# A decoder of scan, depooling and experts: VectorE's side work cut into links and moved ahead of each slot's product

## The reference, cut to what matters

```python
# 1: a selective scan (width 1024, 16 states), per batch
xz = einsum(norm_w * x / rms(x), in_proj_w); xi, z = split(xz)
xc = silu(causal_conv(xi, 4 taps) + conv_b)
dt, Bm, Cm = split(einsum(xc, x_proj_w))
delta = softplus(dt @ dt_proj_w + dt_proj_b)
h_t = exp(delta_t * A) * h_(t-1) + delta_t * Bm_t * xc_t
y = (einsum(h, Cm) + xc * Dp) * silu(z)
x = layernorm(2 * x + y @ out_proj_w)
# 2: depooling of the context (16 x 750 x 1024, its first 512 columns)
x = layernorm(x + rmsnorm(x) @ W_in + b_in + scan over patches of rmsnorm(ctx), at each token's patch)
# 3: a mixture of 8 experts (512 to 2048 to 512), best expert per token, 448 rows each
x = layernorm(x + p * relu(x @ W1) @ W2), rows over the capacity without an expert
```

## Time and profile before

| | |
|---|---|
| median of 3 runs | 2866.54 us (2864.99 to 2867.36) |
| the profiled execution, its own time | 2864.87 us |
| its span, first to last instruction | 2863.1 us |
| VectorE busy (DVE) | 2266.5 us, 79% |
| TensorE busy (PE) | 2575.8 us, 90% |
| ScalarE busy (ACT) | 1704.4 us, 60% |
| GpSimd busy (POOL) | 1426.4 us, 50% |
| mean granted TensorE clock | 0.966 |

### The profile page before, as it was taken

The page is one execution under the profiler, slowest core; times in us unless marked ns, Lnnn a source line. Parts: engine busy times, 40 slices in busy tenths (PEclk is TensorE's granted clock), DMA queues, the critical chain, the costliest instruction groups (busy, mean ns, idle before and its releaser), DMA issues.

```text
span 2863.1 us, 36967 instructions
## 1 busy us (share of the span) xinstructions
PE 2575.8 (90%) x11808; PEld 2143.3 (75%) x11808; DVE 2266.5 (79%) x2456; ACT 1704.4 (60%) x3875; POOL 1426.4 (50%) x868
## 2 busy tenths in 40 slices
PE   4689998989899898989989899998769999999997
PEld 4577877778787776878778787877537888888886
DVE  4899999999999999999999999999933444434442
ACT  2576776867777786767678776767643333233331
POOL 0577667667667766766776766677710100000110
PEclk8799999999999999999999999999978999999999
DMA  7114202022020202212020211202033333343320
GB/s 211 58 39 150 75 17 75 22 74 72 26 82 18 75 17 79 61 38 82 18 74 18 78 52 46 75 17 68 16 124 114 114 117 121 108 139 115 114 101 13
DMA packets 90903, 208.35 MB, mean 73 GB/s; under 512 B 7742, under 2 KB 16574, under 8 KB 90498
## 3 DMA queue, kind: packets, MB, share of 16 engines
q1 hardware_dynamic: 81506, 184.61, 20.7%
q0 software_dynamic: 5120, 14.21, 1.6%
q10 hardware_dynamic: 4096, 7.34, 0.8%
HBM read 176.69 MB, written 29.98 MB: 72 GB/s over the span
## 4 chain that ended last, share of the span: by engine, by line
PE 46%; DVE 25%; issue 15%; POOL 7%; ACT 5%; DMA 1%; SPq 1%; DVEq 0%; POOLq 0%; ACTq 0%
DVE ring L1143 15%; PE ring L1444 12%; PE work L1444 11%; PE work L1277 8%; PE y L1430 7%; POOL arena L884 6%; DVE arena L984 2%; PE work L1256 2%; PE work L1293 2%; DVE arena L1145 2%; ACT ring L748 2%; PE work L1340 1%; DVE arena L944 1%; ACT arena L561 1%; DVE arena L992 1%
## 5 line engine op out<-in xcount | busy, mean ns | idle before, releaser
L884 POOL TENSOR_TENSOR arena<-arena 128x896 f32<-128x896 f32 x512 | 1058.9, 2088 | 581.9 <-PE y L1430 532.3
L1143 DVE TENSOR_TENSOR_SCAN ring<-ring,arena 128x896 f32<-128x896 f32 x512 | 1036.2, 2024 | 27.3 <-ACT ring L748 16.5
L748 ACT ACTIVATE ring<-arena,small 128x224 f32<-128x224 f32 x2048 | 794.5, 436 | 298.1 <-DVE arena L1145 297.6
L1430 PE MATMUL y<-arena,cst_sb 128*128 128x224 f32 x4096 | 868.9, 362 | 105.7 <-DVE arena L1145 105.7
L1430 PEld LDWEIGHTS y<-arena,cst_sb 128*128 128x128 f32 x4096 | 780.1, 194 | 166.2 <-DVE arena L1145 128.7
L1145 DVE TENSOR_TENSOR arena<-ring,arena 128x896 f32<-128x896 f32 x512 | 558.8, 1091 | 17.6
L1256 PE MATMUL work<-arena 128*128 128x224 f32 x1984 | 400.3, 358 | 52.9 <-DVE arena L984 47.1
L1256 PEld LDWEIGHTS work<-arena 128*128 128x128 f32 x1984 | 380.6, 193 | 61.0 <-DVE arena L984 52.6
L1200 DVE SCALAR_TENSOR_TENSOR hidden_lo<-work,hidden_hi 128x448 fp32r<-128x448 f32 x128 | 80.0, 625 | 387.9 <-ACT hidden_hi L788 387.9
L897 POOL DMA_INDIRECT out<-res,ids x32 | 42.7, 1333 | 670.1 <-DVE mst L1185 645.2
L788 ACT ACTIVATE hidden_hi<-work 128x448 fp32r<-128x448 f32 x128 | 69.7, 544 | 422.0 <-PE work L1444 422.0
(11 more groups left out here) (151 smaller groups left out, 2936.3 us busy)
## 6 DMA issues: line engine op xcount, KB each, us to landing
weights<-in_w SPq DMA_DIRECT2D x64, 1024.0 KB, 7.1
arena<-bc_rows SPq DMA_DIRECT2D x128, 448.0 KB, 4.5
arena<-in_ctx SPq DMA_DIRECT2D x16, 896.0 KB, 9.2
expert_rows<-x2e SPq DMA_DIRECT2D x1, 7224.0 KB, 31.9
xrow<-expert_rows SPq DMA_DIRECT2D x8, 903.0 KB, 11.1
arena<-in_xT SPq DMA_DIRECT2D x16, 448.0 KB, 9.5
arena<-in_x SPq DMA_DIRECT2D x16, 448.0 KB, 3.6
out<-arena ACTq DMA_DIRECT2D x32, 224.0 KB, 2.4
```

The source lines that it names most:

```text
L748: last = nc.scalar.activation(decays[s % 2][:, i * L:(i + 1) * L], delta[:, k, :], ACT.Exp, scale=a_neg[:, n:n + 1])
L884: nc.gpsimd.tensor_tensor(u[:, s % 4], dx[:, k:k + 1, :].to_broadcast([P, QN, L]), bc[:, 0, q * QN:(q + 1) * QN, :], ALU.mult).then_inc(u_ ...
L1143: nc.vector.tensor_tensor_scan(h, h, u_flat[:, s % 4, :], 0.0, ALU.mult, ALU.add).then_inc(scan_done, 1)
L1430: last = nc.tensor.matmul(o, ident, u[:, s % 4, i, :], start=False, stop=(q == Q - 1 and i == QN - 1))
```

## The change

1. `woven` gets a third part. On VectorE, `main(s)` is now only the scan; the side work of the slot follows; the product comes last, as `after(s)`.
2. VectorE's side work is cut at more places. Where a piece was a whole chain (`conv0`, `res0`, `norm2.1`, `best`, ...), each link with its wait is now a piece of its own (`conv0.1` to `.3`, `res0.0` to `.2`, `norm21.0` to `.2`, `best.0` to `.4`, ...).
3. All four tables are new, and the banks of `rank`, `dt0`, `t1`, `xatt0`, `xatt1` with them. A full step has VectorE's links in slots 0 to 7, 10 to 19, 21, 25, 26 and 30. ScalarE: the routed rows (`norm2.0`, `norm2.1`) from slots 0 and 3 to 4, silu from 12 to 11, the logarithms from 28 to 30. TensorE: `out0` from slots 7 to 9 to slot 6 whole, `out1` stays at 9. GpSimd: `delta1` and `delta2` to slot 7, `delta3` from 13 to 18, `scatter` from 21 to 24, `ctx` from 15 to 29, `delta0` from 30 to 32.
4. The scaling of the context weights goes from step -1 to slot 3 of step 0. In step -1 ScalarE's `skip` comes before the taps, the first z copies before silu and the squares behind it.
5. Steps 16 and 17 have tables of their own (`PE_DRAIN`, ...), and their jobs are dealt over four banks.

```diff
-        DVE_AT = {"norm2.1": 1, "conv0": 2, "conv1": 3, "conv2": 3.01, "gate3": 3.02, "best": 6, "mask": 6.01, "conv3": 10,
...
+        DVE_AT = {"norm21.0": 0, "norm21.1": 1, "norm21.2": 2, "w_xa": 3, "conv0.1": 3.01, "conv0.2": 3.02, "conv0.3": 3.03,
...
+        PE_DRAIN = in_order("""out0.0 out0.1 tx0 plug out0.2 out0.3 out1.0 out1.1 out1.2 out1.3 tx1 rt t0 rank t1 xatt0.0 xatt0.1
...
+        for s in (NB, NB + 1):
+            last_jobs = sorted(sum(jobs_of[s], []), key=lambda j: FIRST_PART(PE_DRAIN, j))
+            jobs_of[s] = [last_jobs[k::4] for k in range(4)]
...
-        def woven(side, main, scan):
+        def woven(side, main, scan, after=None):
...
                 while due < s + 1:
                     due = next(side, NEVER)
+                if scan and after:
+                    after(s)
...
-            def moments(e, k, h, step_of, name):
-
+            def moments(e, k, h, step_of, name, piece):
+
+                n = e * 8 + 2 * k
+                yield f"{piece}.1"
                 job_copied(dve, step_of, name)
-                n = e * 8 + 2 * k
                 nc.vector.bn_stats(st[:], r[0:H, h]).then_inc(mv_step, 1)
+                yield f"{piece}.2"
                 dve.wait_ge(mv_step, n + 1)
                 apart(dve)
                 nc.vector.bn_aggr(ln[:, k, 0:2], st[:]).then_inc(mv_step, 1)
...
-                dve.wait_ge(tap_ready, nxt * 4 + (j + 1))
-                bank, free = job_full(dve, b, f"xi{j}")
                 n = nxt * 16 + 4 * j
                 for tap in range(1, 4):
+                    yield f"conv{j}.{tap}"
+                    if tap == 1:
+                        dve.wait_ge(tap_ready, nxt * 4 + (j + 1))
+                        bank, free = job_full(dve, b, f"xi{j}")
...
-                    (corrections, pro), (patched, epi), (all_masks, first), (context_weights, first)) if there))
+                    (corrections, pro), (patched, epi), (all_masks, first), (context_weights, isinstance(b, int) and b == 0)) if there))
...
                     nc.vector.tensor_tensor_scan(h, h, u_flat[:, s % 4, :], 0.0, ALU.mult, ALU.add).then_inc(scan_done, 1)
+
+                def product(s):
+                    q = s % Q
+                    g = b * SLOTS + (s + 1)
+                    h = decays[s % 2]
                     dve.wait_ge(scan_done, g)
...
-                woven(side(b, par), main, stages(b)[2])
+                woven(side(b, par), main, stages(b)[2], product)
...
+                if isinstance(step, int) and step == NB and k >= 2 and name == jobs_of[NB][k][0]:
+                    pe.wait_ge(y_done, NB * PAIRS)
```

More of the change, by code:

```diff
@@ L273, in build_decoder @@
                                dt2 dt3 ssq""")
-        ACT_FIRST = in_order("""w_z tap0 tap1 tap2 tap3 square silu z0 z1 z2 z3 xp sp0 sp1 sp2 sp3 logs skip""")
-        DVE_FIRST = in_order("""conv0 w_xa conv1 conv2 conv3 masks0 masks1 masks2 masks3 masks4 masks5 masks6 masks7 corr0 corr1
-                                corr2 corr3""")
+        ACT_FIRST = in_order("""w_z skip tap0 tap1 tap2 tap3 z0 z1 z2 silu square xp z3 sp0 sp1 sp2 sp3 logs""")
+        DVE_FIRST = in_order("""conv0.1 conv0.2 conv0.3 conv1.1 masks0 masks1 conv1.2 conv1.3 conv2.1 conv2.2 conv2.3 conv3.1
+                                conv3.2 conv3.3 masks2 masks3 masks4 masks5 masks6 masks7 corr0 corr1 corr2 corr3""")
+        PE_DRAIN = in_order("""out0.0 out0.1 tx0 plug out0.2 out0.3 out1.0 out1.1 out1.2 out1.3 tx1 rt t0 rank t1 xatt0.0 xatt0.1
+                               xatt0.2 xatt1.0 xatt1.1 xatt1.2""")
+        ACT_DRAIN = in_order("""norm2.0 drop0 tx0 norm2.1 drop1 sq0 sq1 depool tx1 hx0 t0 hx1 t1 exp""")
+        DVE_DRAIN = in_order("""norm21.0 mask gate3 norm21.1 norm21.2 res0.0 patches res0.1 res0.2 res1.0 res1.1 res1.2 best.0
+                                best.1 best.2 best.3 best.4 chance.0 chance.1 slots.0 slots.1 slots.2 slots.3 norm20.0 norm20.1
+                                norm20.2""")
+        POOL_DRAIN = in_order("""ctx scatter""")
         FIRST_PART = lambda at, job: at[job if job in at else job + ".0"]
@@ L732, in logarithms @@
                     logs(b)
-                return together(ACT_AT if not first else ACT_FIRST, *(part() for part, there in (
+                return together(ACT_FIRST if first else ACT_DRAIN if not scan and not pre else ACT_AT, *(part() for part, there in (
                     (rows, tail), (routing, tail), (dropped, tail), (taps, pro), (silus, pro or scan), (channels, pro), (steps, pro),
@@ L870, in next_rows @@
                     nc.gpsimd.tensor_tensor(xn, xT, rinv[:, 1:2, :].to_broadcast([P, DC, L]), ALU.mult).then_inc(xn_ready, 1)
-                return together(POOL_AT, *(part() for part, there in (
+                return together(POOL_DRAIN if not scan and not pre else POOL_AT, *(part() for part, there in (
                     (late_steps, scan), (first_steps, pro), (scatter, tail), (context, epi), (next_rows, pre)) if there))
@@ L1008, in best_expert @@
                 nc.vector.tensor_reduce(rt[:, 0, :], logits, AX, ALU.max).then_inc(rt_step, 1)
+                yield "best.1"
                 dve.wait_ge(rt_step, n + 1)
@@ L1029, in slots_of @@
             def slots_of(b, n):
+                yield "slots.0"
                 bank, free = job_full(dve, b, "rank")
@@ L1127, in patched @@
                     patches(b, e)
-                return together(DVE_AT if not first else DVE_FIRST, *(part() for part, there in (
+                return together(DVE_FIRST if first else DVE_DRAIN if not scan and not pre else DVE_AT, *(part() for part, there in (
                     (masks, epi), (last_gate, epi), (gates, scan), (rows, tail), (convolutions, pro), (routing, tail), (residuals, epi),
-                    (corrections, pro), (patched, epi), (all_masks, first), (context_weights, first)) if there))
+                    (corrections, pro), (patched, epi), (all_masks, first), (context_weights, isinstance(b, int) and b == 0)) if there))
             def body(b, par):
@@ L1407, in next_rows @@
                     squares(b)
-                return together(PE_AT if not (isinstance(b, int) and b == -1) else PE_FIRST, *(part() for part, there in (
+                return together(PE_FIRST if pro and not scan else PE_DRAIN if not scan and not pre else PE_AT, *(part() for part, there in (
                     (inputs, pro), (gate_inputs, pro), (steps, pro), (routing, tail), (outputs, epi), (patches, epi),
```

50 lines of the change are left out of this document (26 added, 24 removed), and 23 rows, old and new, of tables (ACT_AT, DVE_AT, PE_AT).

## The result

The changed kernel takes 2760.13 us (median of 4 runs, 2759.17 to 2767.90) against 2866.51 for the kernel before in the same runs: a ratio of 0.9635, 95% interval 0.9617 to 0.9654. The forecast was 2771 us, range 2750 to 2812. The execution that was profiled is the longest of the four, 2767.90 us with a span of 2766.1. Compared with the one before (2863.1), the 97.0 us that went divide up so: first scan 13.6 earlier; steps 2 to 14 shorter by 71.7; steps 0, 1 and 15 by 1.3; from the end of the last product to the end of the span 10.3 (781.6 to 771.3).

A forecast was written before the change was run, and what follows sets the result against it. VectorE was taken as the bound, TensorE close behind. Thirteen full steps -63, steps 0, 1 and 15 -8, start -13.5, drain -10: 2864.9 - 94.5 = 2770.4, forecast 2771 us; own range 2755 to 2790, 2750 to 2812 with one rival.

The forecast's parts named there:

- Part 1: VectorE in full steps: links between scan and product, and cut chains, save 3.4 us a step, 122.8 to 119.4.
- The place: Links put between scan and product in 22 of 32 slots: 0.11 us each, 2.4 us a full step saved.
- Part 2: VectorE's waits in a full step, for ScalarE, TensorE and GpSimd: reordering cuts them from 3.0 to 1.4 us.
- the routed rows leave slot 0, where the 2.08 us wait is: Slot 0 of a full step: moving ScalarE's routed rows away leaves about 0.3 us of the wait for decays.
- Steps 0, 1 and 15: The three steps with fewer links: -1.5, -2 and -4.5 us, together -8, with the context scaling counted in step 0.
- Start and drain: Before the first scan, 13.5 us earlier (at 88); after the last sums, 10 us earlier, range 6 to 12.
- less 1 where TensorE no longer starts cold: Start, chain from TensorE's second z job to the last softplus: 1 us shorter, ending at 77.6 in place of 78.6.
- The other chain: Start: eight masks, two links, TensorE's second z job, then up to the last softplus; ends at 77.6, the masks' at 77.0.
- The gap can be hidden: Denies a rival: followers start 2.05 us after a scan regardless and cuts save nothing; 2817 us, chance 0.10.
- TensorE didn't take over: Denies a rival: TensorE's idle times of 2.25 and 3.78 us stay, a step can't go below 123.1; 2800 us, chance 0.17.
- it idles there as it does now: Full step: TensorE asks for conv0's bank before conv0 is through and still idles 2.25 us.
- the product is starved: Rival: links ahead of the product, worst at slot 3, delay TensorE, GpSimd and ScalarE; 2908 us, chance 0.04.

The follow-up runs named there:

- e2_product_first: Changed kernel with the product right behind its scan again and the links, still cut and on the new tables, behind the product: 2807.77 us, ratio 0.9791.
- e5_unrolled: Changed kernel with all steps written out, no loop over steps 2 to 11: 2761.59 us, ratio 0.9613.
- e3_weights_in_start: Changed kernel with the scaling of the context weights put back into step -1, behind conv0: 2778.06 us, ratio 0.9686.
- e4_old_drain: Changed kernel with steps 16 and 17 ordered by the common tables and dealt over two banks, as before: 2771.75 us, ratio 0.9666.
- e10_short_links: Kernel before, old tables, side work ahead of the product except in six slots with long pieces (2, 3, 10, 12, 26, 30): 2811.19 us, ratio 0.9806.
- e6_mask_reduce: Kernel before with the copy of a batch's two mask columns exchanged for a reduction over one element: 2841.19 us, ratio 0.9906.

## Why the prediction was right, and where not

The forecast missed the median by 11 us and the profiled execution, against which its sum was made, by 2.5 (2770.4 and 2767.9). Inside that sum some terms are right and others cancel: in steps 2 to 14 VectorE's own work fell by 2.4 us a step more than said, and its waits, which were to fall by 1.6, rose by 0.3. That the total came so near is in part luck.

**Part 1, right in kind, too small.** "Links 1.94 after scan": 1.93. The place gave 2.7 us a step where 2.4 stood. The cuts gave about 1.6 where 1.0 stood. VectorE alone went from 122.8 to 117.0 us (120.33 less 3.35 of waits over 0.2 us), not to 119.4. Of the 2.4 between, 0.3 are the place and 0.6 the cuts, and 1.4 are the mask copy, which I never looked at: its group is small, and its wait is in its duration, not in brackets. The rule of the Trainium skill (VectorE: DVE Perf Modes, The DRAIN you can't avoid) that the semaphore costs nothing doesn't carry over to this pair: it is 2.06 us from a scan to its waiting product and 1.93 to a free link, and over all slots this makes some 40 of the 45 us of `e2_product_first`.

**Part 2, the total near, two of its steps wrong.** Residual 1 waits no more, ScalarE is at most 0.6 late at slot 12 (0.7 said), and the fourth `u` fits. But the waits left are 3.35 us a step and not 1.4. The step "the routed rows leave slot 0, where the 2.08 us wait is" failed: that wait stands at steps 4, 6, 8 and 10 only, the turns of the loop, in both kernels, and it goes with the loop (`e5_unrolled`). I had read it in step 6 alone and put it down to the routed rows, so I took it as all but gone; it grew to 3.0 to 3.4. In the same four steps of this profile the additions at slot 4 wait 1.3 to 1.6 us for ScalarE, which is gone without the loop too. And the 0.4 for `u` "around slot 14" was 0.6 at slot 0, 1.4 to 1.6 at slot 11 and 0.2 at slot 14 in nine steps of thirteen. So the 5.5 us that a step lost are 5.8 less of VectorE's own and 0.3 more of waits, where 3.4 and 1.6 less stood.

**Steps 0, 1 and 15.** -8 said, -1.3 measured: +0.9, -1.9 and -0.3. Step 15 has 3.8 us of waits (for `u`, the decays and the logits) that I left out. Step 0 got 1.2 us from links between scan and product, but paid 1.6 for the scaling and 0.6 for a new wait for `u` at its end.

**Start and drain.** -13.5 said and 13.6 measured, the first scan at 87.7 for 88, by the chain of masks that was laid out; `e3_weights_in_start` gives it back. Only the term "less 1 where TensorE no longer starts cold" was wrong: its second z job took 5.29 us, at a granted clock of 0.60, where before it took 4.84. The other chain was done 1.4 us before 77.6 all the same, and the masks decided. -10 said for the drain: 9.9 at the last addition, 10.3 to the end; `e4_old_drain` gives 9 back.

```profile
51.09 5.29 PE L1290 MATMUL work<-arena 128*128 128x224 f32 x16 [16.28 <-DVE arena L1006]
```

**The rivals.** The gap can be hidden. TensorE didn't take over, though what is left is partly its doing. Both of the idle times on which that rival rested went, and so did the prediction's own "it idles there as it does now": over steps 2 to 14 TensorE waited for products and for the convolutions, as the first two lines have it before; in the changed kernel the third and fourth are its longest waits, and it has none for a convolution.

```profile
PE y L1430 <- DVE arena L1145: 59.4, 30, 3.9
PE work L1256 <- DVE arena L984: 24.5, 13, 2.2
```

```profile
PE work L1274 <- ACT arena L589: 21.5, 13, 1.8
PE y L1464 <- DVE arena L1177: 11.7, 26, 0.9
```

That the product is starved was no empty rival: on the old tables it is what happens, 33 us slower, at the very place named (slot 3, long pieces of the convolutions). The changed kernel pays less for it: it too has twelve additions ahead of the product of slot 3, but no other slot holds more than 2.3 us of links. Whether slot 3 would do better with the product first, as in `e10_short_links`, wasn't tried with the new tables.

## What to carry to other kernels

Put a short instruction that depends on neither between an instruction and its waiting follower: it hides the follower's wait, here some 0.12 us a time. Ask first who waits for the follower: with short pieces alone ahead of it the old order ran 56 us faster (some 12 of them by the mask copy), with the long ones too 33 us slower. Look for waits that wear another form: an instruction whose duration has two values, and a wait that stands in every second step only. Look at the same slot in all steps before putting a wait down to one piece.

## What the runs showed of the hardware

A VectorE copy of 112x2 took 0.16 us or up to 2.08, as far as the end of GpSimd's running multiplication; the reduction in its place 0.14 to 0.15 always, also with GpSimd running.

The waits in a step go with TensorE's clock. In the kernel before, TensorE idles 3.8 us at the same place of each of the thirteen steps. Behind it the eight sums take 3.36 us in step 13, at a granted clock of 0.50 (1.2 of 2.4 GHz), and 1.78 in step 7, at full clock. In `e6_mask_reduce` both come behind an idle 2.35; in the changed kernel, step 6, the clock fell to 0.53 a few us behind an idle 1.75. Windows of the kernel before, the same 27 us (18 to 45 into the step) of steps 7, 8 and 9, with clock 1.00, 0.94 and 0.87:

```profile
979.70:1006.70 27.00, 22.82 (x119) 1.00 0.00 1
1105.06:1132.06 27.00, 23.11 (x117) 0.94 0.00 1
1231.14:1258.14 27.00, 22.82 (x107) 0.87 0.00 1
```

Residual 1 behind them waits 0, 1.60 and 2.93 us for the output projection. In the changed kernel the same windows of steps 7 and 8 have 1.00 and 0.87, and the wait is 0.61 for ScalarE (slot 12) or 1.39 for `u` (slot 11). It goes with the clock in all thirteen steps of the profiles of both kernels; what decides between the values from step to step stays open, and no run forced one.

```profile
968.88 2.03 DVE L1170 TENSOR_TENSOR_SCAN ring<-ring,arena 128x896 f32<-128x896 f32 x1 [0.61 <-ACT ring L765]
...
1088.62 2.03 DVE L1170 TENSOR_TENSOR_SCAN ring<-ring,arena 128x896 f32<-128x896 f32 x1 [1.39 <-POOL arena L901]
```

At a turn of the loop VectorE stands some 2.4 us longer than at slot 0 of other steps, and TensorE stands 1.8 to 2.2 us there for no cause that the profile shows. With all ten steps written out 8.5 us were gained and 5.0 lost elsewhere, why is open; four steps a turn brought 7.5 us to the median.
